# A Mamba block beside a mixture of experts: z projections between dt projections, and eight buffers for the products with C

## The chip, the cores and the metric

One core of one Trainium2 chip. The metric is the time in microseconds (us) of one execution on the device, the median of the runs. Engines by their names in the profile: PE (TensorE, matmuls), PEld (its weight loads), DVE (VectorE), ACT (ScalarE), POOL (GpSimd), SP (SyncE, which issues most of the transfers).

## What is computed

Input x is 2 x 512 tokens of 256 values. With xn the normalised x, the output is x + mamba(xn) + moe(xn), all in fp32.

```python
xz = xn @ in_proj_w.T                      # 1024 columns
x, z = split(xz)                           # 512 channels each
u = silu(conv4(x) + conv_b)
dt, Bm, Cm = split(u @ x_proj_w.T)         # 128, 16, 16 columns
dt = softplus(dt @ dt_proj_w.T + 2 * dt_proj_b)
h[l, n] = exp(dt[l] * A[n]) * h[l-1, n] + dt[l] * Bm[l, n] * u[l]    # 16 states n
y = (sum_n h[l, n] * Cm[l, n] + u * D) * z
mamba = y @ out_proj_w.T

p = softmax(xn @ gate_w.T)                 # 64 experts, the best 8 of each token
moe = sum over the 8 of p_e * (silu(xn @ w1_e.T) * (xn @ w3_e.T)) @ w2_e.T
```

## The kernel before

The 512 channels of the two sequences make 8 groups g of 128 channels by 512 steps (G = 8). Each group has 16 states, and a state is one scan over a 128x512 tile. Experts are worked in 128 tiles of 128 slots: tokens are scattered to their slots in slot_x, each tile is multiplied with its expert's weights, results go to slot_y and are gathered back. The order on each engine is written by hand, and engines wait for counters (semaphores) that other engines raise; `then_inc` raises one as an instruction ends, `wait_ge` waits. Some counters start C = 2 (or, cb_ok, K = 8) high.

**Head.** Norm, router, input projection, convolution, then u. GpSimd scatters 64 pieces of 128 rows from x_sb to slot_x by indirect transfers (L308). SP loads B and C rows into bc (L232) and then the first weight tiles (L242).

**dt and z.** TensorE computes eight dt projections (L850, banks 4 to 7, dt_ps counts them), two records of the trace each, then waits for the last of them to be used, then eight z projections (L858, also banks 4 to 7, four records each; z_ps counts each). ScalarE does for each group Abs (L667), Exp (L669) and a sum "+ 1" (L671), later Ln (L674), then it copies z to SBUF (L678), waiting for z_ps (L676) and for VectorE's softplus counter sp_v (L677), and after that begins the decays exp(dt A) of group 0 (`decay`, L687). VectorE does the maximum with zero (`over_zero`, L463), a rounding correction (`rounded`, L467) and three steps a group of `softplus` (L471, L473, L475).

**Group 0.** VectorE runs a scan (L501), forms the next state's input (`spread_u`, L494) and the product of the state with C (`times_c`, L508) for each state (`pair0`). TensorE adds the products into bank 0 with an identity matrix (`sum_states`, L872) and raises acc_ok by one for each. There are two product buffers, so L506 waits in each state for acc_ok of the state two before. After 14 sums and the last z copy TensorE goes on to the experts (`tile_slot`).

**Groups 1 to 5 beside the experts.** Expert tiles run through TensorE, ScalarE (tanh L710, copies L701, L704) and VectorE (`hidden`, L523 and L526), scans run between them, and GpSimd forms inputs (L316) and adds products in pairs (hp, L323). SP loads weights (`load_w`, L242) into the eight buffers w_buf and tokens (`load_x`, L245) into x_buf. The first x load waits until the whole scatter has landed (scat).

**Groups 6 and 7 (the tail).** VectorE goes back to `pair0` with two buffers. GpSimd gathers 64 pieces from slot_y (L349); from tile 4 on it waits for cb_ok. ScalarE builds eight diagonal matrices of weights a tile (L778, each behind cb_ok) and copies finished outputs (`output`, L766). TensorE sums states, combines the gathered rows with the diagonals (`combine`, L963, cb_ok counts each matmul) and does the output projection (L968). `finish_group` (L514, L516) waits for all 16 sums of a group. At the very end VectorE combines the last 128 tokens in eight steps (L629).

## Time and profile before

| | us |
|---|---|
| median of 3 runs | 599.52 |
| the three runs | 599.52, 605.4, 594.88 |
| span of the profiled execution | 596.5 |
| busy in that span: PE, DVE | 439.8, 452.3 |
| busy: POOL, ACT | 301.8, 271.5 |

The page gives the profiled execution's span, from the first to the last instruction, and no other time of its own; the median of the runs lies 3.0 us above the span. Times in the rows below count from the span's start. Busy time of POOL includes its indirect transfers' issue. "remote", "another core or an unknown queue" and "issue" stand where the profile can't name who ended a wait.

### The profile page before, as it was taken

How to read it: one execution, taken by the hardware profiler on the slowest of the kernel's cores; microseconds unless marked ns; L12 is line 12 of the kernel's file. 1: busy time of each engine (PE TensorE's matmuls, PEld its weight loads, DVE VectorE, ACT ScalarE, POOL GpSimd, SP SyncE). 2: the span in 40 equal slices, each digit the busy share in tenths (PEclk: the TensorE clock that was granted, in tenths of full speed). 3: DMA queues.
4: the chain of work that ended last, by engine and by line, in shares of the span. 5: the costliest groups of instructions: out<-in, count | busy, mean ns of one | idle time of the engine just before them, and what ended most of it. 6: DMA issues, size and time to landing. Idle time of an engine off the chain costs nothing.

```text
span 596.5 us, 10167 instructions
## 1 busy us (share of the span) xinstructions
PE 439.8 (74%) x2116; PEld 304.9 (51%) x2116; DVE 452.3 (76%) x870; ACT 271.5 (46%) x668; POOL 301.8 (51%) x260
## 2 busy tenths in 40 slices
PE   2987856200768888788889888899989958268888
PEld 2632222000115766667677776687777725135555
DVE  5476478001999999999989999788888889259786
ACT  1334690003223555555556666466555623134443
POOL 2003777771004555555554341667767667737750
PEclk9978967755677999999999999899999979768989
DMA  8995797423003899988989899699989443313331
GB/s 303 427 425 238 245 405 268 151 106 110 14 0 115 267 271 279 297 268 283 276 286 294 277 293 300 211 294 304 331 271 327 148 150 103 100 53 106 101 93 35
DMA packets 71642, 131.65 MB, mean 221 GB/s; under 512 B 7584, under 2 KB 44704, under 8 KB 69568
## 3 DMA queue, kind: packets, MB, share of 16 engines
q1 hardware_dynamic: 65472, 114.56, 57.7%
q0 software_dynamic: 6144, 16.79, 8.7%
q8 instruction: 11, 0.18, 0.1%
q14 instruction: 15, 0.12, 0.1%
HBM read 88.00 MB, written 43.32 MB: 220 GB/s over the span
## 4 chain that ended last, share of the span: by engine, by line
DVE 29%; PE 24%; issue 19%; another core or an unknown queue 9%; POOL 7%; ACT 7%; DVEq 2%; DMA 2%; POOLq 1%; SPq 0%; ACTq 0%
DVE bank L501 13%; POOL hp L323 5%; DVE hc L508 5%; PE bank L872 3%; PE bank L897 3%; PE bank L906 3%; DVE gt L523 3%; PE bank L808 2%; PE bank L914 2%; POOL dbu L316 2%; PE bank L968 2%; PE bank L963 2%; DVE wdt L526 2%; ACT dA L687 1%
## 5 line engine op out<-in xcount | busy, mean ns | idle before, releaser
L501 DVE TENSOR_TENSOR_SCAN bank<-dA,dbu 128x512 f32<-128x512 f32 x128 | 173.8, 1358 | 52.8 <-ACT dA L687 43.5
L316 POOL TENSOR_TENSOR dbu<-dtu,bc 128x512 f32 x80 | 102.0, 1276 | 173.4 <-DVE bank L501 162.0
L687 ACT ACTIVATE dA<-dt_sb,a_neg 128x512 f32 (+1 forms) x128 | 93.3, 729 | 92.9 <-DVE bank L501 62.7
L872 PE MATMUL bank<-hc,ident 128*128 128x512 f32 x92 | 64.8, 794 | 72.3 <-DVE hc L508 52.0
L508 DVE TENSOR_TENSOR hc<-bank,bc 128x512 f32<-128x512 f32 x128 | 87.6, 685 | 32.0 <-remote 20.6
L308 POOL DMA_INDIRECT slot_x<-x_sb,slot x64 | 64.0, 1000 | 68.8 <-DMA slot_x<-bc 49.6
L701 ACT COPY x_sb<-bank 128x256 f32<-128x256 f32 x128 | 47.7, 373 | 104.0 <-PE bank L906 87.7
L323 POOL TENSOR_TENSOR hp<-hc 128x512 f32<-128x512 f32 x41 | 67.3, 1642 | 3.9 <-DVE hc L508 3.8
L872 PEld LDWEIGHTS bank<-hc,ident 128*128 128x128 f32 x92 | 18.5, 232 | 99.3 <-DVE hc L508 73.7
L897 PE MATMUL bank<-x_sb,wring 128*128 128x128 f32 x512 | 68.1, 276 | 0.0
L897 PEld LDWEIGHTS bank<-x_sb,wring 128*128 128x128 f32 x512 | 62.7, 193 | 0.0
L906 PE MATMUL bank<-wring,wdt 128*128 128x256 f32 x128 | 40.6, 399 | 22.0 <-DVE wdt L526 21.3
L704 ACT COPY x_sb<-bank 128x256 f32<-128x256 f32 x128 | 48.4, 378 | 0.1
L526 DVE SCALAR_TENSOR_TENSOR wdt<-gt,bank 128x128 f32<-128x128 f32 x128 | 37.0, 289 | 13.5
L710 ACT ACTIVATE th<-bank 128x128 f32<-128x128 f32 x128 | 35.5, 278 | 20.1 <-PE bank L897 19.8
L914 PE MATMUL bank<-hp,ident 128*128 128x512 f32 x82 | 42.9, 606 | 1.1 <-POOL hp L323 1.1
L906 PEld LDWEIGHTS bank<-wring,wdt 128*128 128x128 f32 x128 | 21.7, 192 | 36.5 <-issue 33.1
L523 DVE SCALAR_TENSOR_TENSOR gt<-th,bank 128x128 f32<-128x128 f32 x128 | 35.2, 275 | 2.2 <-ACT th L710 2.0
L858 PE MATMUL bank<-xT,win 128*128 128x512 f32 x32 | 20.9, 817 | 18.8 <-issue 18.8
L897 PE MATMUL bank<-x_sb,win 128*128 128x128 f32 x256 | 34.7, 280 | 0.0
L897 PE MATMUL bank<-x_sb,xT 128*128 128x128 f32 x256 | 33.8, 275 | 0.0
L494 DVE TENSOR_TENSOR dbu<-dtu,bc 128x512 f32<-128x512 f32 x48 | 32.4, 675 | 0.5 <-DVE dtu L475 0.5
(137 smaller groups left out, 709.7 us busy)
## 6 DMA issues: line engine op xcount, KB each, us to landing
wring<-w_moe SPq DMA_DIRECT2D x64, 384.0 KB
slot_y<-x_sb SPq DMA_DIRECT2D x65, 256.0 KB, 4.8
slot_x<-bc SPq DMA_DIRECT2D x16, 1024.0 KB, 22.2
xT<-w_moe SPq DMA_DIRECT2D x32, 384.0 KB, 4.1
win<-w_moe SPq DMA_DIRECT2D x31, 384.0 KB, 4.6
bc<-bc_dram SPq DMA_DIRECT2D x8, 1024.0 KB
xg<-slot_x SPq DMA_DIRECT2D x32, 256.0 KB, 4.7
xT<-slot_x SPq DMA_DIRECT2D x16, 256.0 KB, 4.8
```

Of the source, the lines that this page charges most:

```text
L308: pool.indirect_dma_start(slot_x, bass.IndirectOffsetOnAxis(ap=slot[:, t * K + k:t * K + k + 1], axis=0), x_sb[:, t, :], None).then_inc(sc ...
L316: nc.gpsimd.tensor_tensor(dbu[:, j], at(dtu, g), bc[:, bass.ds(n, 1), 0].rearrange("p a l -> p (a l)"), ALU.mult).then_inc(dbu_ok, 1)
L323: nc.gpsimd.tensor_tensor(hp[:], hc[:, 0], hc[:, 1], ALU.add).then_inc(hp_ok, 1)
L501: nc.vector.tensor_tensor_scan(H[:], dA[:, j], dbu[:, j], 0.0, ALU.mult, ALU.add).then_inc(scan_ok, 1)
L508: nc.vector.tensor_tensor(hc[:, j], H[:], bc[:, bass.ds(n, 1), 1].rearrange("p a l -> p (a l)"), ALU.mult).then_inc(hc_ok, 1)
L523: nc.vector.scalar_tensor_tensor(gt[:], th[:, j], 1.0, GU[j][:, 0:INTER], ALU.add, ALU.mult).then_inc(gt_ok, 1)
L526: nc.vector.scalar_tensor_tensor(hh[:, w], gt[:], 0.5, GU[j][:, INTER:2 * INTER], ALU.mult, ALU.mult).then_inc(hh_ok, 1)
L687: nc.scalar.activation(dA[:, j], at(dt_sb, g), ACT.Exp, scale=a_neg[:, bass.ds(g, 1), bass.ds(n, 1)].rearrange("p a l -> p (a l)")).then_i ...
L872: nc.tensor.matmul(Y_ACC[:], ident[:], hc[:, j], start=first, stop=True, skip_group_check=True).then_inc(acc_ok, 1)
L897: mm = nc.tensor.matmul(GU[1 - j][:, half * P:(half + 1) * P], w_buf[w][:, k * 2 * P + half * P:k * 2 * P + (half + 1) * P], xTs[:, 1 - j, ...
L906: nc.tensor.matmul(YT[:, 0:DM], hh[:, w % 4], w_buf[w][:, WGU:], start=True, stop=True).then_inc(ye_ok, 1)
L914: nc.tensor.matmul(Y_ACC[:], ident[:], hp[:], start=(g is not None), stop=True, skip_group_check=True).then_inc(acc_ok, 2)
```

## The change

1. z projections are put between the dt projections: after dt 0 to 3, TensorE does z 0, dt 4, z 1, dt 5, z 2, dt 6, z 3, dt 7, then z 4 to 7. They go to banks 0, 1, 2, 3, 1, 2, 4, 5. z_ps is raised for z 0 to 3 one by one, and once, by four, after z 7.
2. ScalarE copies z 0 to 3 behind the Exp of groups 4 to 7, and z 4 to 7 behind the decays of states 2 to 5 of group 0. The "+ 1" sum goes from ScalarE to VectorE (`plus_one`). ScalarE starts group 0's decays after softplus of groups 0 and 1. The exponentials sp_e live in dA and in the weight ring, since z_sb keeps their old place.
3. Eight product buffers in groups 0, 6 and 7. In group 0 they are six parts of the weight ring and the two of hc; at the end hc, xg, prob, mask, key and a part of the ring. TensorE raises acc_ok by four after every fourth sum. VectorE waits for acc_ok once in four states (states 8 and 12 of groups 0 and 6, every fourth of group 7), for the sum four to eight states back. The loops over pairs in groups 6 and 7 are unrolled.
4. SP's first four weight loads wait for z_ps (their buffers are now the first ones of xT and win), and weight load 4 waits for the 14 sums of group 0.
5. The diagonals are doubled (two sets of eight), so ScalarE builds a tile's diagonals behind cb_ok of the tile two before. VectorE and ScalarE wait for the experts' last results before group 6 uses xg and the ring.

```diff
+        w_all = wring[:].rearrange("p a b -> p (a b)")
+        diag = w_all[:, 0:2 * K * P].rearrange("p (k q) -> p k q", k=2 * K)
+        whole = [w_all[:, i * L:(i + 1) * L] for i in range(6)]
+        sp_e = [dA[:, 0], dA[:, 1]] + whole
+        hc_first = whole + [hc[:, 0], hc[:, 1]]
...
-        w_buf = [wring[:, i] for i in range(4)] + [f[:, i * WCOL:(i + 1) * WCOL] for f in free for i in range(2)]
+        w_buf = [f[:, i * WCOL:(i + 1) * WCOL] for f in free for i in range(2)] + [wring[:, i] for i in range(4)]
...
+            sp.wait_ge(z_ps, G)
             for i in range(4):
                 load_w(i, i, False)
-            sp.wait_ge(z_ps, G)
+            sp.wait_ge(acc_ok, NS - 2 + C)
             load_w(4, 4, False)
...
+            def plus_one(g):
+                dve.wait_ge(sp_x, g + 1)
+                nc.vector.tensor_scalar(sp_l[:, g], sp_e[g], 1.0, None, ALU.add).then_inc(sp_s, 1)
...
-            def times_c(g, n, j, alone=True):
+            def times_c(g, n, j, ring=None):
                 s = g * NS + n
-                if alone:
-                    dve.wait_ge(acc_ok, s + C - 1)
                 dve.wait_ge(scan_ok, s + C + 1)
...
-            def pair0(g, q, count, after=None):
+            def pair0(g, q, count, ring, after=None):
                 for j in range(2):
                     n = 2 * q + j
+                    if n % PART == 0 and (n >= RING or g == G3):
+                        dve.wait_ge(acc_ok, g * NS + n - RING + PART + C)
...
+            dve.wait_ge(t_ok, TILES)
+            dve.wait_ge(ye_ok, TILES + 2 + C)
+            pair0(G2, 0, NS, hc_end)
...
-                act.wait_ge(sp_x, g + 1)
-                nc.scalar.activation(sp_l[:, g], sp_e[:, g], ACT.Copy, bias=1.0).then_inc(sp_s, 1)
+                if g >= 4:
+                    keep_z(g - 4)
...
-            act.wait_ge(sp_v, SP_STEPS * G)
+            act.wait_ge(sp_v, SP_STEPS * 2)
...
             for n in range(NS):
                 decay(0, n, n % 2)
+                if 2 <= n < 6:
+                    keep_z(n + 2)
...
+                        if t:
+                            act.wait_ge(cb_ok, (t - 1) * K + k + 1)
+                        nc.scalar.activation(diag[:, t % 2 * K + k], ident[:], ACT.Copy, scale=c8[:, t, k:k + 1]).then_inc(dg_ok, 1)
...
+            def project_z(g):
+                d, b = g % DT, g // DT
+                if g == 2:
+                    pe.wait_ge(bc_row, 1)
+                if g == 3:
+                    pe.wait_ge(split, 2)
+                if 4 <= g < 6:
+                    pe.wait_ge(z_ok, g - 2)
+                if g >= 6:
+                    pe.wait_ge(dt_max, g - 1)
...
+                if g < 4:
+                    mm.then_inc(z_ps, 1)
+                if g == G - 1:
+                    mm.then_inc(z_ps, 4)
+            for g in range(4):
+                project_dt(g)
+            for g in range(4):
+                project_z(g)
+                project_dt(4 + g)
+            for g in range(4, G):
+                project_z(g)
...
+                mm = nc.tensor.matmul(Y_ACC[:], ident[:], ring[n % RING], start=(n == 0), stop=True, skip_group_check=True)
+                if count:
+                    mm.then_inc(acc_ok, count)
             for n in range(NS - 2):
-                sum_states(0, n, n % 2, n == 0)
+                sum_states(0, n, hc_first, PART if n % PART == PART - 1 else 2 if n == NS - 3 else 0)
```

## Rows read from the trace of the kernel before

**Rows 1.** The chain that ended last, 82 to 150 us: start, length, what.

```profile
101.47 9.82 issue
...
111.31 11.14 another core or an unknown queue
...
141.40 2.08 another core or an unknown queue
```

**Rows 2.** The timeline: start us, length us, engine, line; in brackets idle time before, releaser.

```profile
82.41 13.39 PE L858 MATMUL bank<-xT,win 128*128 128x512 f32 x24 [6.41 <-issue]
...
100.08 0.59 ACT L678 COPY xpad<-bank 128x512 f32<-128x512 f32 x1 [9.92 <-remote]
...
111.93 3.71 PE L858 MATMUL bank<-xT,win 128*128 128x512 f32 x4 [7.43 <-issue]
```

**Rows 3.** The timeline of DVE from its first softplus step to its first scan.

```profile
84.93 0.69 DVE L471 TENSOR_TENSOR dtu<-dtu,xpad 128x512 f32<-128x512 f32 x1 [1.32 <-ACT dtu L674]
...
101.99 0.69 DVE L494 TENSOR_TENSOR dbu<-dtu,bc 128x512 f32<-128x512 f32 x1 [0.53 <-DVE dtu L475]
146.21 1.23 DVE L501 TENSOR_TENSOR_SCAN bank<-dA,dbu 128x512 f32<-128x512 f32 x1 [43.53 <-ACT dA L687]
```

**Rows 4.** Line 308, the scatter: shortest, median, longest ns; first and last start us.

```profile
L308 POOL DMA_INDIRECT slot_x<-x_sb,slot x64: 959/963/1630, 53.3 to 135.6; - x64
```

**Rows 5.** The timeline where the experts begin, 144 to 189 us.

```profile
144.21 0.34 SPq L242 DMA_DIRECT2D xT<-w_moe  x1
...
181.71 2.07 PE L872 MATMUL bank<-hc,ident 128*128 128x512 f32 x2 [0.47 <-DVE hc L508]
...
188.37 0.27 DVE L523 SCALAR_TENSOR_TENSOR gt<-th,bank 128x128 f32<-128x128 f32 x1
```

**Rows 6.** The timeline of the tail, 481 to 590 us.

```profile
481.03 1.23 DVE L501 TENSOR_TENSOR_SCAN bank<-dA,dbu 128x512 f32<-128x512 f32 x1 [1.15 <-POOL hp L323]
...
507.98 1.13 PE L872 MATMUL bank<-hc,ident 128*128 128x512 f32 x2 [0.42 <-issue]
...
519.86 0.69 DVE L508 TENSOR_TENSOR hc<-bank,bc 128x512 f32<-128x512 f32 x1 [10.09 <-remote]
...
588.73 4.12 DVE L629 SCALAR_TENSOR_TENSOR x_sb<-dtu,c,x_sb 128x256 f32<-128x256 f32 x8
```

**Rows 7.** DVE's waits, 481 to 588 us: us in total, times, longest us.

```profile
DVE hc L508 <- remote: 20.6, 3, 10.1
```

**Rows 8.** The timeline of the first dt projections.

```profile
65.11 4.53 PE L850 MATMUL bank<-hc,wdt 128*128 128x512 f32 x10
```

**Rows 9.** Groups of lines, 66 to 102.5 us: count, busy us, mean ns, idle before.

```profile
L463 DVE TENSOR_SCALAR dt_sb<-bank,dtb 128x512 f32<-128x512 f32 x8 | 6.0, 750 | 6.3 <-issue 6.3
...
L467 DVE SCALAR_TENSOR_TENSOR xpad<-dtu,xpad 128x512 f32<-128x512 f32 x8 | 5.4, 682 | 0.0
...
L671 ACT ACTIVATE dtu<-xpad 128x512 f32<-128x512 f32 x8 | 5.0, 630 | 0.3
```

**Rows 10.** DMA issues: KB each, median us from issue to landing.

```profile
xg<-slot_x SPq DMA_DIRECT2D x32, 256.0 KB, 4.7
```

**Rows 11.** The timeline of GpSimd's scatter.

```profile
86.02 1.17 POOL L308 DMA_INDIRECT slot_x<-x_sb,slot  x1 [0.30 <-issue]
...
102.59 0.96 POOL L308 DMA_INDIRECT slot_x<-x_sb,slot  x1 [0.30 <-issue]
...
126.67 0.96 POOL L308 DMA_INDIRECT slot_x<-x_sb,slot  x1 [0.30 <-issue]
```

**Rows 12.** GpSimd's gathers in 482 to 581 us, two of four rows.

```profile
L349 POOL DMA_INDIRECT xT<-slot_y,slot_r x16 | 18.1, 1131 | 14.8 <-PE bank L963 8.7 <-issue 4.3 <-DVE dbu L494 1.8
...
L349 POOL DMA_INDIRECT dt_sb<-slot_y,slot_r x16 | 15.7, 981 | 4.9 <-issue 4.9
```

**Rows 13.** The timeline of GpSimd's gathers, ten of them.

```profile
497.43 0.95 POOL L349 DMA_INDIRECT win<-slot_y,slot_r  x1 [0.30 <-issue]
...
508.70 1.24 POOL L349 DMA_INDIRECT dt_sb<-slot_y,slot_r  x1 [0.30 <-issue]
```

83 lines of the change are left out of this document (40 added, 43 removed).

## The prediction

> **What bounds the kernel now.** I read the chain of waits first, then the timeline of single engines where the chain names no releaser, then grouped rows for prices. The span is 596.5 us, and the median of three runs is 599.5 us; I work on the span and add the 3.0 us between the two at the end.
>
> The chain has a hole at the front. From 101.47 to 143.5 us it is made of five waits ahead of ScalarE's z copies (L678), four of them put down to an unknown queue [rows 1]. The timeline shows what is waited for. TensorE had six of the eight z projections done by 82.41 + 13.39 = 95.8 us, the last at 111.93 + 3.71 = 115.6 us; the copies after the second start at 100.08, 111.29, 122.48, 132.28, 141.37 and 143.50 us, nine to eleven us apart until the last one (three of the five pieces of the chain stand in rows 1) [rows 1, 2]. ScalarE waits at L676 for z_ps, which TensorE counts up, and L677's counter, VectorE's, stood complete at 101.5 us. So a count that TensorE owed at 92 to 96 us is seen 19 to 36 us late. VectorE had all its softplus work done at 101.5 and its first dbu ready at 102.7, and then stood 43.5 us until the first decay (L687), which ScalarE issues behind the copies [rows 3]. What works in those 43.5 us is GpSimd's scatter, whose 64 transfers run from 53.3 to 136.6 us [rows 4]. SP too sat on z_ps, for weight load 4, until 144.21 [rows 5].
>
> The same thing comes back in the tail. Groups 6 and 7 run from 481.03 us at one state per 2.54 us, while GpSimd gathers. VectorE's product (L508) waits three times, 20.6 us in all, the longest 10.09 us with TensorE's matmul (507.98 + 1.13 us) long over [rows 6, 7]. L506 waits there for acc_ok, again a count of TensorE's. Between the two, from 188 to 481 us, the change touches nothing.
>
> **The change part by part.** I take as the mechanism that, once GpSimd's indirect transfers have run for 26 (tail) to 39 us (front), counts that TensorE sends are seen about 10 us late, one after the other. Counts of the first 30 us of the scatter (the dt projections from 65.11 us on) were prompt [rows 8].
>
> Step 1, z between dt. A dt projection is two records at 0.45 us each (ten records in 4.53 us) at a granted clock near full; a z projection is four, so 1.8 us, or 3.7 us at half clock [rows 2, 8]. Four z's between the eight dt's end dt 7 at about 65.1 + 8 x 0.9 + 4 x 1.8 = 79.5 us, where its Abs is due at about 80, so it costs 0. At half clock it is 65.1 + 8 x 1.8 + 4 x 3.7 = 94, some 11 us later than the softplus can bear; I take full clock, since TensorE would have no gap to lose it in, and keep 11 us as bound. All eight z's then end at 87 to 90 us, inside the time in which counts were prompt. ScalarE loses eight sums of 0.63 us and gains four copies of 0.59; VectorE gains the eight sums, at most 0.68 us each like its other pass [rows 2, 9]. VectorE then has 8 x (0.75 + 0.68 + 0.68) = 16.9 us of work from 67.0 us, with a start-up gap of 1.3, thus 85 us; its first softplus step began at 84.93 before [rows 3]. Zero.
>
> Step 2, group 0 moves forward. The decays wait for two softplus groups only, and four z copies are laid behind decays 2 to 5, where ScalarE is idle for over a microsecond in each state. The first scan then starts at 102.7 instead of 146.21 us. State 13's sum started 181.71 - 146.21 = 35.5 us after the first scan [rows 3, 5]; so now at 138.2, done at 140.3.
>
> Step 3, late counts in group 0. Eight buffers and one count in four states: state 8 needs the count of state 3. That matmul ends at about 114; with the 10.6 us of the z copies it is seen at 124.8 against a need at 102.7 + 8 x 2.54 = 123.0. States 12 and 7 meet likewise. I charge 3 us in all (bounds 0, and 2 x 11 us if the counts queue behind others). State 13 is summed by 143.3.
>
> Step 4, the start of the experts. They need the scatter complete, state 13's count on SP (new), then weight load 4 and x loads: 0.4 + 0.5 us of issue and 4.7 us to land [rows 5, 10]. The scatter runs at 1.267 us a transfer with VectorE idle (102.59 to 126.67, 19 steps) and at 1.381 beside the softplus (86.02 to 102.59, 12 steps) [rows 11]. 26 transfers beside the scans cost 26 x 0.114 = 3.0 us: the last lands at about 141. After it the counts are prompt within 2 us, as for the last z copy [rows 2], so SP goes on at 145 and x is there at 150.5. The first gate product (L523) follows the transposes by 1.8 us: 152.3. It started at 188.37 before, held then by VectorE's own group 0 [rows 5]. Gain 36 us. Bounds: 40 if no count is late (148.2), 27 if state 13's count takes a full 11.2 us. SP's four first weight loads move behind z_ps; they were 8.4 us apart before and are needed at 150, so 34 us from 90 fit.
>
> Beside the scatter's pace the Trainium skill, SBUF — State Buffer, section "SBUF: two separate sides", has a rule against this change: while VectorE runs a two-port mode, GpSimd can't write the descriptors of its transfers. The moved sum (tensor_scalar, fp32, SBUF to SBUF) may be of that kind. By the rule eight such instructions hold up the scatter by their own length, 8 x 0.68 = 5 us; by the pace of rows 11 it is 8 x 0.114 = 0.9 us, and the sum holds neither.
>
> Step 5, the tail. Without the 20.6 us of waits on acc_ok and some 1 us of small ones the last eight-step sum (L629) could start at 588.73 - 21.6 = 567.1 [rows 6]. GpSimd then becomes the limit: 64 gathers, in four rows of 16, are 18.1 + 17.3 + 16.4 + 15.7 = 67.5 us of work and 4.3 + 4.9 + 4.6 + 4.9 = 18.7 us of issue [rows 12], so 482.84 + 86.2 = 569.0, and 1.4 us to land as the scatter's last: 570.4. At its fast pace, 1.25 us (497.43 to 508.70, nine steps) [rows 13], it would be 564. I take 570.4: gain 18.3. What stays late: ScalarE still waits four times for cb_ok ahead of output copies (L774) and VectorE for acc_ok in finish_group, each with only two states, 5 us, of slack against a count that can be 10 us late; five spots, late at the rate of three in 32 states, 5 us each, make 2.3; I charge 3. Gain 15 (bounds: 5 if most of the 20.6 us only moves to those spots, 21 if nothing is late and the gathers keep their fast pace). The unrolled loops and the doubled diag cost nothing: group 0 was unrolled before and keeps 35.5 / 14 = 2.54 us a state, as the loops do; diag gains four states of slack. The waits for ye_ok and t_ok ahead of group 6 are met at 480.0, before GpSimd's hp sum, which held the scan until 481.03 [rows 6].
>
> Sum: 36 + 15 = 51; 596.5 - 51 = 545.5 of span, 548.5 us. What measurement of this kernel tells from no change is about 2%, 12 us.
>
> **The rivals.**
> (a) The counts queue. If TensorE's counts pass one in 10 us while GpSimd's transfers run, eight combine counts and one acc count per four states pile up in the tail, and group 0 waits at 8 and at 12. For it: the even distance of the z copies [rows 1]. Against it: only three late counts were waited for in 100 us of tail, which has over 90 of them [rows 7]. Front gain 27, tail 8: 564.5 us.
> (b) It is not TensorE's count that is late but ScalarE and VectorE that are held by the scatter. Then group 0 can't run beside it, the front gains nothing, the tail stays or gains its 18: 581 to 599 us. Against it: VectorE worked through its softplus to 101.5 us at full pace beside the scatter, and copies were late when z_ps was their only open wait. In a sentence apart: the Trainium skill, TensorE: Matmul & The Clock Gate, section "The cost: per-tile semaphore tail", puts counts that queue up at 26 ns each; by that figure fewer counts save 2 us here at most and (b) is what is left, yet the trace shows 9 to 11 us each.
> (c) It ends slower: GpSimd's issue is thinned out by a VectorE that never pauses, to one transfer per state, 2.54 us. The scatter's last 26 transfers then take 26 x (2.54 - 1.38) = 30 us more, and 64 gathers take 163 us instead of 86, 77 more: 548.5 + 30 + 77 = 655.5 us. It decides from a pace of about 1.95 us (at p us a transfer the gains are 176 - 90 p). Against it: the nine steps at 1.25 us stood beside scans at full cadence [rows 13].
> (d) Half clock in step 1: softplus 11 us later, first scan at 113.6, state 13 summed at 151 and promptly counted, x at 157. Gain 30: 554.5, inside the forecast's own range.
>
> **How the numbers follow.** Forecast 548.5 us, own range 540 to 560, chance 0.62, (d) included. (a) 0.20, to 568. (b) 0.07. (c) 0.03. Left over 0.08, mostly below 540. The range 538 to 568 takes the bounds 40 + 21 = 61 us and 27 + 5 = 32 us of gain and leaves out (b), (c) and a little. Faster by over 2%: 0.94; within: 0.03; slower: 0.03.
>
> **What would show it.** Right: first scan at about 103 us; the four late z copies at single spots of group 0; scatter over by about 140; first gate product at 150 to 155; from there to the first scan of group 6 the same 292.7 us; no wait over 3 us at the products; last gather at about 569, L629 close behind. Step 3 is wrong if state 8 or 12 waits for over 5 us; step 4 if x is there well before or after 150; step 5 if output copies or combine hold ScalarE, or GpSimd's gaps grow. The whole is wrong if the first scan still waits for the scatter's end.

## The result, and the profile after

| | kernel before | changed kernel |
|---|---|---|
| median | 598.36 us (4 executions, 594.88 to 605.40) | 572.75 us (4 executions, 567.82 to 586.70) |
| profiled execution | span 596.5 | 567.82, span 565.9 |
| first scan of group 0 | 146.21 | 104.03 |
| first gate product | 188.37 | 163.62 |
| first scan of group 6 | 481.03 | 458.00 |
| last eight-step sum of rows (L629, now L648) | 588.73 | 558.17 |

The ratio is 0.9531, 95% interval [0.9447, 0.9615]: 4.7% faster, where 8.5% was forecast (548.5 us), and the median lies above the range of 538 to 568. Ratios leave out executions more than 1.5% above the fastest one of the same kernel; since such executions turn out to be part of the story, the range of all of them stands beside each median.

The profiled execution is the fastest of the four; no profile shows where the others lost the 3 to 19 us more. Of the 51 us forecast it has 30.6 (596.5 - 565.9): 24.8 at the front (188.37 - 163.62) instead of 36, 7.5 in the tail (107.7 - 100.2) instead of 15, and 1.7 lost in the middle (292.7 and 294.4 us). So the missing 20 us are 11.3 at the front, 7.5 in the tail and 1.7 between.

The front of the changed kernel, timeline (start, length, engine, line; in brackets the idle time before and its releaser):

```profile
73.98 1.02 PE L875 MATMUL bank<-hc,wdt 128*128 128x512 f32 x2
74.84 7.03 PE L890 MATMUL bank<-xT,win 128*128 128x512 f32 x16
...
120.24 2.04 PE L916 MATMUL bank<-wring,ident 128*128 128x512 f32 x2 [5.26 <-DVE wring L523]
```

```profile
81.37 0.69 ACT L691 ACTIVATE wring<-bank,dtb 128x512 f32<-128x512 f32 x1 [5.93 <-issue]
...
101.93 1.28 ACT L707 ACT_TABLE_LOAD   x1 [13.15 <-DVE dtu L487]
...
116.39 0.58 ACT L686 COPY xpad<-bank 128x512 f32<-128x512 f32 x1 [10.29 <-remote]
```

```profile
104.03 1.23 DVE L517 TENSOR_TENSOR_SCAN bank<-dA,dbu 128x512 f32<-128x512 f32 x1 [1.05 <-issue]
...
117.69 1.23 DVE L517 TENSOR_TENSOR_SCAN bank<-dA,dbu 128x512 f32<-128x512 f32 x1 [6.17 <-issue]
...
138.80 1.23 DVE L517 TENSOR_TENSOR_SCAN bank<-dA,dbu 128x512 f32<-128x512 f32 x1 [7.30 <-issue]
...
163.62 0.29 DVE L538 SCALAR_TENSOR_TENSOR gt<-th,bank 128x128 f32<-128x128 f32 x1 [2.93 <-ACT th L732]
```

Read them by pairs. The last dt projection ended at 75.0, and ScalarE's Abs of it started at 81.37, 5.93 us after ScalarE had come to it: 6.4 us behind its sum. The last z ended at 81.87 (74.84 + 7.03) and its copy started at 116.39: 34.5 us behind. ScalarE's copy holds the decay behind it, so the fourth scan stands 6.17 us. State 3's sum ended at 122.28 and state 8's scan, which waits for its count, started at 138.80: 16.5 us behind. The z copies that held the kernel before for 43.5 us [rows 1 to 3] are gone, but late counts now stop the front at three places. It isn't the waiting engine that is slow. SP waits for the same count of z 7, and its first instruction behind that wait, the value load of L246, starts at the same instant as ScalarE's copy (the view of line 246: shortest, median and longest ns; first and last start):

```profile
L246 SPq TENSOR_LOAD <-tile_e x127: 263/272/960, 116.4 to 439.1; - x127
```

SP's queue in the timeline:

```profile
121.25 8.42 SPq L249 DMA_DIRECT2D xT<-w_moe  x2
136.66 7.72 SPq L249 DMA_DIRECT2D win<-w_moe  x2
156.85 0.34 SPq L249 DMA_DIRECT2D wring<-w_moe  x1
157.25 0.93 SPq L252 DMA_DIRECT2D xg<-slot_x  x2
```

Weight load 4 waits for state 13's count and the x load (L252) is issued behind it, at 157.25, though the scatter had been over since 140.8 (its last transfer, 139.00 + 1.79). SP's queue is the chain by which 14.8 us of stopped scans become a late expert.

The tail, waits from 458 us on (total, times, longest), and the timeline where they stand:

```profile
ACT x_sb L789 <- remote: 18.2, 2, 11.6
...
DVE bank L517 <- ACT dA L707: 10.9, 2, 8.0
...
DVE u L529 <- PE bank L916: 5.1, 1, 5.1
```

```profile
505.88 0.37 ACT L789 COPY x_sb<-bank 128x256 f32<-128x256 f32 x1 [11.60 <-remote]
...
540.35 0.37 ACT L789 COPY x_sb<-bank 128x256 f32<-128x256 f32 x1 [6.59 <-remote]
```

The first line reads: ScalarE stood 18.2 us in all ahead of L789, in two waits, the longest 11.6 us. VectorE's 20.6 us at the products [rows 7] are gone. What is late next are two output copies, 18.2 us of ScalarE, of which 10.9 reach the scans, and the last sum's count, 5.1.

### The profile page after: what moved, and what is told of

Its sections match the earlier page's. It is cut to its first block, busy times and chain, and to the rows that moved or that the text cites. A ratio compares the mean times of both kernels' runs of the same rounds, so it can differ in the third digit from the quotient of the medians.

```text
span 565.9 us, 10023 instructions
## 1 busy us (share of the span) xinstructions
PE 429.2 (76%) x2116; PEld 300.2 (53%) x2116; DVE 453.1 (80%) x878; ACT 264.8 (47%) x660; POOL 302.8 (54%) x260
## 4 chain that ended last, share of the span: by engine, by line
DVE 32%; PE 24%; issue 17%; ACT 9%; DMA 4%; another core or an unknown queue 3%; POOL 3%; SPq 3%; DVEq 2%; ACTq 0%; POOLq 0%
DVE bank L517 12%; PE bank L943 5%; PE bank L952 5%; DMA slot_y<-x_sb 3%; ACT dA L707 3%; DVE gt L538 3%; POOL hp L331 3%; PE bank L960 3%; DVE dbu L510 2%; PE bank L1009 2%; DVE hc L523 2%; PE bank L832 2%; DVE wdt L541 2%; DVE wring L523 2%
## 5 line engine op out<-in xcount | busy, mean ns | idle before, releaser
L324 POOL TENSOR_TENSOR dbu<-dtu,bc 128x512 f32 x80 | 101.8, 1274 | 143.4 <-DVE bank L517 132.0
L316 POOL DMA_INDIRECT slot_x<-x_sb,slot x64 | 67.0, 1047 | 70.1 <-DMA slot_x<-bc 50.8
L723 ACT COPY x_sb<-bank 128x256 f32<-128x256 f32 x128 | 47.6, 372 | 102.5 <-PE bank L952 86.1
L523 DVE TENSOR_TENSOR hc<-bank,bc 128x512 f32<-128x512 f32 x92 | 63.1, 686 | 9.0 <-POOL hp L331 8.8
L943 PE MATMUL bank<-x_sb,wring 128*128 128x128 f32 x512 | 69.8, 281 | 0.0
L943 PEld LDWEIGHTS bank<-x_sb,wring 128*128 128x128 f32 x512 | 64.5, 198 | 0.0
L916 PE MATMUL bank<-wring,ident 128*128 128x512 f32 x32 | 27.7, 963 | 44.6 <-issue 33.9
L952 PE MATMUL bank<-wring,wdt 128*128 128x256 f32 x132 | 42.7, 406 | 15.8 <-DVE wdt L541 14.8
L916 PEld LDWEIGHTS bank<-wring,ident 128*128 128x128 f32 x32 | 7.2, 274 | 62.4 <-issue 52.7
L952 PEld LDWEIGHTS bank<-wring,wdt 128*128 128x128 f32 x132 | 22.7, 196 | 30.6 <-issue 25.4
L952 PE MATMUL bank<-win,wdt 128*128 128x256 f32 x64 | 20.7, 405 | 15.7 <-DVE wdt L541 15.4
```

Source lines behind the costliest of these rows:

```text
L316: pool.indirect_dma_start(slot_x, bass.IndirectOffsetOnAxis(ap=slot[:, t * K + k:t * K + k + 1], axis=0), x_sb[:, t, :], None).then_inc(sc ...
L324: nc.gpsimd.tensor_tensor(dbu[:, j], at(dtu, g), bc[:, bass.ds(n, 1), 0].rearrange("p a l -> p (a l)"), ALU.mult).then_inc(dbu_ok, 1)
L523: nc.vector.tensor_tensor(ring[n % RING] if ring else hc[:, j], H[:], bc[:, bass.ds(n, 1), 1].rearrange("p a l -> p (a l)"), ALU.mult).the ...
L943: mm = nc.tensor.matmul(GU[1 - j][:, half * P:(half + 1) * P], w_buf[w][:, k * 2 * P + half * P:k * 2 * P + (half + 1) * P], xTs[:, 1 - j, ...
L952: nc.tensor.matmul(YT[:, 0:DM], hh[:, w % 4], w_buf[w][:, WGU:], start=True, stop=True).then_inc(ye_ok, 1)
```

## The experiments

Each kernel ran beside the kernel before, on the same chip. Where texts of the first batch number their theories, 1 is that TensorE's counts are held while GpSimd's indirect transfers run (later, in its strict form with one count leaving after the other, Q), and 3 that a TensorE that idles sends its counts late. This table of the profiled executions carries most of what follows. "Middle" is from the gate product to group 6, "tail" from there to the last sum of rows (us).

| kernel | first scan | gate product | middle | tail |
|---|---|---|---|---|
| before | 146.2 | 188.4 | 292.7 | 107.7 |
| changed | 104.0 | 163.6 | 294.4 | 100.2 |
| e1_z_one | 113.6 | 168.5 | 294.1 | 100.3 |
| e2_hold_scatter | 98.2 | 226.5 | 293.7 | 98.8 |
| e3_front_alone | 99.9 | 151.4 | 296.1 | 105.2 |
| e4_tail_alone | 144.3 | 186.4 | 295.9 | 99.0 |
| e5_acc_each (no late count) | 99.8 | 146.3 | 295.1 | 87.5 |
| e6_z_late (no late count) | 100.8 | 146.4 | 296.1 | 87.5 |
| e7_scatter_pause (no late count) | 99.7 | 153.3 | 294.2 | 87.5 |
| e8_out_late (no late count) | 101.1 | 148.2 | 294.7 | 87.5 |
| f1_after_again (the changed kernel) | 140.3 | 184.6 | 293.6 | 100.2 |
| f2_combined | 101.9 | 152.1 | 297.3 | 96.1 |
| g1_dt_first | 107.3 | 182.0 | 297.1 | 99.3 |
| g2_dt_combined | 97.4 | 151.9 | 295.1 | 100.7 |
| g3_many_counts | 97.2 | 154.6 | 296.0 | 102.3 |
| g4_dt_pause | 100.0 | 155.0 | 296.7 | 99.3 |
| h1_before_pause | 101.8 | 154.3 | 296.0 | 112.0 |
| h2_pauses_combined | 99.8 | 149.2 | 296.8 | 99.1 |
| i1_more_stops | 100.4 | 152.8 | 296.5 | 99.4 |
| i2_after_stops (the kernel of e7) | 100.8 | 153.1 | 294.9 | 99.9 |

The middle is within 5 us everywhere; all is decided in front and tail.

**e1_z_one.** Is it the size of the raise (four at once behind z 7)?

```
-                if g == G - 1:
-                    mm.then_inc(z_ps, 4)
+                if g == G - 1:
+                    mm.then_inc(z_ps, 1)
```
(with waits for 5 instead of 8.)

> The changed kernel, but the count after z 7 is one instead of four (ScalarE, SP and GpSimd wait for 5). In the changed kernel the last z matmul ended at 81.9 us and the count was seen at 116.3 us, 34.4 us late; a raise by four may be worked off as four raises of 8.6 us. Theory 1 (TensorE's raises pass one at a time, 8 to 11 us each, while GpSimd's indirect transfers run, and a raise by four is four of them): the copy of z 4 starts by about 92 to 106 us, right behind its decay, the 6.2 us gap of VectorE ahead of state 3 goes, and the time falls by 4 to 8 us against the changed kernel. Theory 2 (a raise is late by itself, whatever its size): the copy still starts at about 116 us, time as the changed kernel within 2 us.

573.58 us (569.35 to 585.83), ratio 0.9546 [0.9499, 0.9593]: as the changed kernel. z 4's copy still waited 12.51 us, to 128.91. The size of a raise is not the cause.

**e2_hold_scatter.** The scatter waits until group 0 has been summed.

```
             pool.wait_ge(rt, RT_SLOT)
+            pool.wait_ge(acc_ok, NS - 2 + C)
```

> The changed kernel, but GpSimd begins its scatter only when the 14 sums of group 0 are counted. Theory 1 (counts are late because of GpSimd's indirect transfers): z 4's copy starts right behind decay 2, all 16 states of group 0 follow each other at 2.54 us with no gap over 0.5 us, state 8 waits for nothing. The scatter then runs from about 140 to 222 us, so the whole takes 60 to 70 us longer than the changed kernel, about 635 us. Theory 3 (a count of TensorE's is late because TensorE stands idle behind it): the copy of z 4 is again some 30 us behind the last z matmul and state 8 waits again, with no transfer of GpSimd's in flight.

628.75 us, since the experts start 38 us later than before. But in front nothing is late: the dt copies wait 0.5 and 0.8 us, the scans start at 98.17 and run through, although TensorE idles as before. So an idle TensorE is not enough for a late count, and with GpSimd's transfers gone the late counts went too. It is one execution; h1 below rests on four. Nor is it the load of the DMA engines as such: in e2 they were busy throughout from 70 to 80 us (387 GB/s), beside dt counts in time, and in the changed kernel z 7's count stayed out from 90 to 110 us while they were busy for 26 to 36%.

**e3_front_alone and e4_tail_alone.** The change cut in two: e3 keeps the tail of before (two buffers, a count for each sum, one set of diagonal matrices), e4 is the kernel before with the tail's three edits.

```
e3 +        hc_end = 4 * [hc[:, 0], hc[:, 1]]
e3 +                if ring is hc_end:
e3 +                    dve.wait_ge(acc_ok, s + C - 1)
...
e4 +                mm = nc.tensor.matmul(Y_ACC[:], ident[:], ring[n % RING], start=(n == 0), stop=True, skip_group_check=True)
e4 +                if count:
e4 +                    mm.then_inc(acc_ok, count)
```

> The changed kernel with the tail as before: two product buffers and a count per state in groups 6 and 7, one set of diagonals. The profiles of before and after put 24.8 us of the gain in front of the first gate product and 7.5 us behind the first scan of group 6. If the parts add up: about 24 us under the kernel before, 7 us over the changed kernel, with late waits of 15 to 22 us at the products of the tail. If the front's gain is given back later: within 10 us of the kernel before.

> The kernel before with only the tail of the change: eight product buffers, a count in four states and doubled diagonals in groups 6 and 7. If the parts add up: 7 to 8 us under the kernel before; the products wait for nothing, and the late counts show at the output copies of ScalarE instead (two waits, 18 us in the changed kernel) and at the decays. If the ring alone did what was forecast: 15 us or more under.

e4 took 591.93 us (589.55 to 594.67), 0.9877 [0.9837, 0.9918]: the tail is worth some 8 us, with the same two output copies in the way (18.2 us, the longest 11.6). Its front is that of before, and so are its z copies, timelines of TensorE and ScalarE:

```profile
81.72 15.19 PE L870 MATMUL bank<-xT,win 128*128 128x512 f32 x28 [6.41 <-issue]
```

```profile
102.36 0.59 ACT L688 COPY xpad<-bank 128x512 f32<-128x512 f32 x1 [10.62 <-issue]
...
133.86 0.59 ACT L688 COPY xpad<-bank 128x512 f32<-128x512 f32 x1 [9.92 <-remote]
```

Seven z projections (28 records) were over at 96.9 us. The copies of z 3 to z 6 started at 102.36, 112.86, 123.36 and 133.86: four counts that TensorE owed by 96.9 were seen one at a time, 10.5 us apart. e3 took 579.97, but from 562.30 to 601.17, and in its profiled execution (562.30) the front had almost no late count at all: gate product at 151.4, as forecast for the whole change (152.3). The executions of this one kernel lie up to 39 us apart; what was late in the slower ones no profile shows.

**e5_acc_each, e6_z_late, e7_scatter_pause, e8_out_late.** One edit each on the changed kernel: a count per state in group 0 with a wait for state n - 8 alone; z 4 to 7 copied behind decays 10 to 13; three stops in the scatter; output copies a tile later.

```
e5 -                sum_states(0, n, hc_first, PART if n % PART == PART - 1 else 2 if n == NS - 3 else 0)
e5 +                sum_states(0, n, hc_first, 1)
e6 -                if 2 <= n < 6:
e6 -                    keep_z(n + 2)
e6 +                if 10 <= n < 14:
e6 +                    keep_z(n - 6)
e7 +                if t in (2, 4, 6):
e7 +                    pool.wait_ge(scat, 16 * t * K)
e8 -                    if i == 1 and 1 <= t <= 4:
e8 -                        act.wait_ge(cb_ok, t * K + K)
e8 -                        output(t - 1)
e8 +                    if i == 0 and 2 <= t <= 5:
e8 +                        act.wait_ge(cb_ok, t * K)
e8 +                        output(t - 2)
```

> Group 0 of the changed kernel with TensorE's count raised once per state again (16 counts instead of four); state n from 8 on waits for the sum of state n - 8 alone, not for a group of four. Theory Q (counts of TensorE leave one at a time, about one per 10 us, while GpSimd's indirect transfers run, so each further count makes the later ones later): after z 7's count at about 116 the counts of states 0, 1, 2 come at about 126, 136, 140 to 143, so VectorE stops at states 9 to 11 for 10 us or more in all, and the first gate product comes no earlier than 163. Theory L (a count is late by some time, up to 16 us here, however many there are): the sum of state n - 8 has then 20 us of slack in place of 12.7, VectorE's 7.3 us wait ahead of state 8 goes, ScalarE's wait for z 7 stays, and the first gate product comes at 156 to 158; time 564 to 569 us.

> The changed kernel with ScalarE's four copies of z 4 to 7 behind the decays of states 10 to 13 instead of 2 to 5: nothing of the scans stands behind z 7's count before 130 us. If the late z count cost what the trace shows (6.2 us of scans), VectorE runs on until state 8; there it waits for the count of state 3's sum. If that count comes by its own time (theory L, some 16 us behind its sum, which now ends at about 114), at 130: state 8's scan would stand at about 124.5, so 5 us of waiting and a first gate product at 155 to 157. If it comes when GpSimd's transfers end (139, theory E), state 8 waits 14 us and the gate product stays at 162 to 164: no gain. SP's weight loads behind z 7's count stay late in both. Time 564 to 568 by L, 572 by E.

> The changed kernel with GpSimd waiting, ahead of its 17th, 33rd and 49th indirect transfer, until all earlier ones have landed: three stops of some 2 to 3 us, the scatter's end at 146 to 149 instead of 141. If counts of TensorE pass when GpSimd stops (as they do in the tail, where eight of them land within 0.4 us, 3 us behind GpSimd's stop), z 7's count comes at about 100 and the sum of state 3's is at hand for state 8: ScalarE's 10.3 us and VectorE's 7.3 us waits shrink to under 2 us each, the scans end at about 146, and the scatter's end sets x: first gate product at 155 to 158, time 564 to 569 us. If they don't pass in so short a stop, both waits stay and the end of the scatter adds to them: gate product at 164 or later.

> The changed kernel with ScalarE's output copies of tiles 0 to 3 one tile of states later in the tail (behind the decay of state 4t + 10 in place of 4t + 7 or so: slack of seven states in place of four, 7.6 us more; the two projections that need the bank follow two states later). If the copy's wait for late counts is what holds the scans in the tail (VectorE's 8.0 and 2.9 us), it shrinks to 0 to 4 us in all and the tail from the first transfer of the gather to the last multiply by z is 7 to 11 us shorter: time 562 to 566 us. If another wait takes its place at once (the diagonal matrices' own for the counts, with one state less of slack, or GpSimd's for free rows), it moves under 3 us: 570 to 573 us.

None of these expectations came true, for a reason that none had: in the four profiles of this batch no count was late, and the kernel before took 536.57 us (24 executions, 534.15 to 539.39) instead of 599. The changed kernel itself was not in this batch, but three kernels one edit away from it: e5, e6 and e8 took 538.52, 538.24 and 538.94, ratios 1.0028, 1.0030 and 1.0029 (each interval within 1.000 to 1.006). The scans of e5_acc_each, timeline of VectorE:

```profile
99.79 1.23 DVE L517 TENSOR_TENSOR_SCAN bank<-dA,dbu 128x512 f32<-128x512 f32 x1 [1.05 <-ACT dA L710]
...
137.92 1.23 DVE L517 TENSOR_TENSOR_SCAN bank<-dA,dbu 128x512 f32<-128x512 f32 x1
141.72 2.02 DVE L517 TENSOR_TENSOR_SCAN bank<-dA,dbu 128x512 f32<-128x512 f32 x1 [1.84 <-ACT dA L710]
146.32 0.29 DVE L538 SCALAR_TENSOR_TENSOR gt<-th,bank 128x128 f32<-128x128 f32 x1 [2.58 <-ACT th L735]
```

Sixteen scans at 2.54 us with no gap, then the scatter's end. So all that can be measured of the change's gain, it gains on late counts; where there are none, these three are 0.3% behind the kernel before. The batch ran on a chip on which a later batch (i1, i2) had the kernel before at 606 us: the lateness is a property neither of a chip nor of the program alone. What switches it on I can't say. e7's stops were 5.0, 1.7 and 1.7 us, and it took 543.21 us, 4.7 more than e5.

**f1_after_again and f2_combined.** The changed kernel once more, and the edits of e5, e6 and e8 together.

> The changed kernel, nothing edited, once more beside the kernel before. The last four kernels ran with the kernel before at 536.6 us, 62 us under the time it had in the first two batches, and no count of TensorE was late in any of their profiles; the lateness belongs to something outside the program. If this batch's chip has late counts (kernel before near 598), the changed kernel takes 568 to 576. If it has none (kernel before near 537), VectorE runs without a stop from the first scan to the last in both kernels, the change takes nothing off its path and the two are within 0.5%: 535 to 540.

> The edits of three kernels together, on the changed kernel: one count per state in group 0 with the wait for state n - 8 alone, ScalarE's copies of z 4 to 7 behind the decays of states 10 to 13, output copies one tile later in the tail. Where counts are late: by theory L (a count is late by a time of its own) the front loses 6 and 7 us of waits and the tail 7 to 11, 550 to 557 us against 568 to 576 of the changed kernel. By theory Q (counts leave one by one, 10 us apart, while GpSimd's transfers run) the sixteen counts of group 0 stop VectorE at states 9 to 11 and the front gains nothing: 562 to 568. Where no count is late: 535 to 540, as without the edits.

f1 took 588.12, 586.92, 586.10 and 556.60 us: the same kernel is 11 to 13, or 43, us faster than before (599.45). f2: 554.08, then 572.68, 574.09 and 585.14. The profiled execution of f1 is the slowest (588.12); timeline of ScalarE:

```profile
83.62 0.69 ACT L691 ACTIVATE wring<-bank,dtb 128x512 f32<-128x512 f32 x1 [10.13 <-remote]
97.62 0.69 ACT L691 ACTIVATE wring<-bank,dtb 128x512 f32<-128x512 f32 x1 [12.18 <-remote]
114.43 0.69 ACT L691 ACTIVATE wring<-bank,dtb 128x512 f32<-128x512 f32 x1 [14.98 <-remote]
137.66 1.28 ACT L707 ACT_TABLE_LOAD   x1 [15.84 <-DVE dtu L487]
```

These are the Abs of dt 5, 6 and 7, whose sums ended at 71.5, 74.1 and 76.7 us: counts 12, 24 and 38 us late, seen one at a time, 14 and 17 us apart, with the first scan at 140.32. The softplus of all groups stands behind them, and the decays behind that. The kernel before had no such wait in its profile: its dt counts were all raised ahead of any z. In f2's profiled execution they were on time (one of 3.2 us), and no scan of states 1 to 15 waited over 1.2 us.

**g1_dt_first to g4_dt_pause.** g1 undoes the interleaving, with what hangs on it: z 3 raises z_ps by four, and ScalarE copies z 0 to 3 ahead of the decays. g3 adds seven counts to it, on a counter that nobody waits for; g4 adds stops; g2 adds f2's edits. The cut shows the order on TensorE and the line of g3.

```
g1 -        Z_BANK = [PS[i] for i in (0, 1, 2, 3, 1, 2, 4, 5)]
g1 +        Z_BANK = PS[0:G]
...
g1 -            for g in range(4):
g1 -                project_dt(g)
g1 -            for g in range(4):
g1 -                project_z(g)
g1 -                project_dt(4 + g)
g1 -            for g in range(4, G):
g1 -                project_z(g)
g1 +            for g in range(G):
g1 +                project_dt(g)
g1 +            for g in range(G):
g1 +                project_z(g)
g3 +                    if g > 3 and k < KD - 1:
g3 +                        mm.then_inc(spare, 1)
```

> The changed kernel with one part undone: the eight dt projections first, the eight z behind them (each z with a bank of its own, one count of four behind z 3 and one behind z 7; ScalarE copies z 0 to 3 ahead of the decays and z 4 to 7 behind decays 2 to 5 as in the change). Theory Q (late counts leave in order, one every 5 to 15 us, from some point between 68 and 80 us on): with only the dt counts ahead, dt 7's is at hand by 73, no copy of a dt projection waits, the scans start at about 100 in every run, and the spread of the changed kernel (556 to 588) goes: all runs at 555 to 572. Theory S (the spread comes from somewhere else, interleaving z has no part in it): times of 556 to 588 again, and Abs waits of 6 to 15 us in some profiles. Where no count is late: 536 to 541.

> dt first as in g1_dt_first, with the three edits of f2_combined (a count per state in group 0, z 4 to 7 copied behind decays 10 to 13, output copies one tile later). f2_combined had 554.1 in the execution whose dt counts were in time and 573 to 585 in the others. Theory Q: here all are of the first sort, 548 to 556. Theory S: 554 to 585 again.

> g1_dt_first with seven more counts: each of the eight matmuls of z 4 to 7 but the last also raises a semaphore that nobody waits for. Theory Q: the seven stand ahead of z 7's count in the queue, which then comes when the scatter ends (141 or later) instead of between 90 and 120; ScalarE's copy of z 4 waits to then, VectorE stops after state 3, and the first gate product is 20 us or more later than in g1_dt_first: 580 to 600 us. Theory L (a count is late by a time of its own, whatever number is raised): no difference from g1_dt_first. Where no count is late: 536 to 541.

> g1_dt_first with GpSimd waiting ahead of its 17th, 33rd and 49th scatter transfer until all earlier ones have landed. On a chip without late counts the same stops were 5.0, 1.7 and 1.7 us and cost 5 to 7 us. If held counts pass in such a stop, ScalarE's wait for z 7 and VectorE's ahead of state 8 are under 3 us each, and the end of the scatter (147 to 149) sets x: first gate product at 155 to 158. If they don't pass, both waits stay as in g1_dt_first, and it is slower than that by 3 to 8 us.

g1: 562.58 us, but 556.41, 558.21 and 562.58 beside 587.76 and 588.11, so the spread stayed, against theory Q as I had put it. No Abs of a dt projection waited over 1.1 us in its profile; there (588.11) z's two counts took over, timelines of TensorE and ScalarE:

```profile
73.76 13.90 PE L888 MATMUL bank<-xT,win 128*128 128x512 f32 x32
```

```profile
103.09 2.05 ACT L686 COPY xpad<-bank 128x512 f32<-128x512 f32 x4 [19.16 <-remote]
143.01 0.59 ACT L686 COPY xpad<-bank 128x512 f32<-128x512 f32 x1 [33.68 <-remote]
```

z 7 had ended at 87.7 and its count came at 143.0, behind the scatter's last transfer, 55 us late, though only two counts were raised for all eight z. g3, with seven more raised ahead of z 7's, should have been worse. It took 562.00 (558.80 to 562.93), and the copy of z 4 stood 1.1 us:

```profile
100.40 0.58 ACT L686 COPY xpad<-bank 128x512 f32<-128x512 f32 x1 [1.11 <-remote]
```

The count had come 16 us late (z 7 ended at 84.4). It came 16.4 us behind z 3's (the copies behind that started at 84.03), with the seven in between. So counts do not pass at a fixed 10 us each, and theory Q falls as I had put it. What stays open is whether a counter with nobody waiting counts in full here. VectorE also stood 10.97 us in this profile, at 139.76, for a sum's count. g4, with stops: 560.55, all four within 560.20 to 563.49, and no late count in front; its gate product (155.0) waits for the scatter's end. g2: 557.06 (554.53 to 560.15), 0.9285 [0.9205, 0.9364], with more slack in place of stops, and none of its executions is among the late ones either.

**h1_before_pause.** The kernel before, and only GpSimd's three stops:

```
             for t in range(NT):
+                if t in (2, 4, 6):
+                    pool.wait_ge(scat, 16 * t * K)
                 for k in range(K):
```

> The kernel before with one edit: GpSimd waits ahead of its 17th, 33rd and 49th scatter transfer until all earlier ones have landed. g4_dt_pause had no late count in the front at all with these stops. If held counts pass in each stop, and none is held for some 15 us behind one, the five copies of z that each waited about 10 us [the stretch from 88 to 144 us of the kernel before] come within 25 us: first scan at 112 to 125 instead of 146, first gate product at 155 to 168 instead of 188, time 567 to 580 us: with two lines of the kernel changed, most of what the whole change brought. If stops help only where few counts are in use (the kernel before has 8 of z and 16 of group 0, each waited for at once), 590 to 600. On a chip without late counts: 537 to 543.

572.50 us (571.11 to 573.98), 0.9511 [0.9446, 0.9577]: with two lines, what the whole change brought (0.9531), and steadier (four executions within 2.9 us, where the changed kernel's lay 19 us apart). GpSimd's stops, and the places where the kernel before had stood 43.5 us, timeline:

```profile
81.13 1.32 POOL L310 DMA_INDIRECT slot_x<-x_sb,slot  x1 [5.04 <-DMA slot_x<-x_sb,slot]
...
104.52 1.90 POOL L310 DMA_INDIRECT slot_x<-x_sb,slot  x1 [1.71 <-DMA slot_x<-x_sb,slot]
```

```profile
90.52 0.58 ACT L680 COPY xpad<-bank 128x512 f32<-128x512 f32 x1 [1.13 <-DVE dt_sb L475]
92.24 0.58 ACT L680 COPY xpad<-bank 128x512 f32<-128x512 f32 x1 [1.13 <-PE bank L860]
```

```profile
149.54 2.39 DVE L503 TENSOR_TENSOR_SCAN bank<-dA,dbu 128x512 f32<-128x512 f32 x1 [7.46 <-issue]
154.34 0.29 DVE L525 SCALAR_TENSOR_TENSOR gt<-th,bank 128x128 f32<-128x128 f32 x1 [2.40 <-ACT th L712]
```

The z copies are 1.7 to 2.1 us apart, the pace of TensorE's projections and VectorE's softplus, where they were 10 [rows 1]. The first scan is at 101.82, two us ahead of the changed kernel's, and the gate product at 154.34, nine ahead. This is the cleanest proof that the unbroken run of transfers is the cause. Whether a stop helps because GpSimd pauses or because no transfer of its is then on the way, no run separates. One stop at 76 to 81 us is enough for all z counts to 98 us to be prompt. Its tail, which has no stop, is as before or worse (112.0), with one product waiting 15.56 us.

**h2_pauses_combined, i1_more_stops, i2_after_stops.** h2 is g2 with one stop in the scatter and two in the gather; i1 is g2 with two and five; i2 is the changed kernel with the scatter's three, the same kernel as e7_scatter_pause. The cut shows the stops in the gather.

```
h2 +                if t in (2, 6):
h2 +                    pool.wait_ge(g_ld[1], (t // 4 + 1) * 16 * K)
i1 +                if t in (2, 3, 5, 6, 7):
i1 +                    pool.wait_ge(g_ld[(t - 1) % 4], ((t - 1) // 4 + 1) * 16 * K)
```

> g2_dt_combined with three stops of GpSimd: one in the scatter (ahead of its 33rd transfer) and two in the gather of the tail (ahead of the 17th and the 49th), each until the earlier transfers have landed. g2_dt_combined's tail from the first transfer of the gather to the last sum of rows was 98.9 us, 85.7 on a chip without late counts. If stops of 2 to 5 us release the counts held in the tail, VectorE's 6.5, 1.7 and 6.4 us waits there go and the tail is 89 to 94 us; the stop in the scatter costs its 2 to 3 us at the front: 549 to 554 us. If the end of the gather sets the tail, its stops add to it: 558 to 563.

> g2_dt_combined with stops of GpSimd ahead of the 17th and 33rd transfer of the scatter and ahead of each tile of the gather from the third on. In h2_pauses_combined a count raised at 488.9 passed at 506.0, with GpSimd's next stop: here a stop comes every 10 to 12 us of the gather, so no wait on a late count is over 10 us and the 13.3 us one goes; five stops of 2 us put the gather's end at 90 to 94 us behind its start. Tail from its first transfer to the sums of rows 90 to 95 us (h2_pauses_combined: 97.3), time 546 to 552 us. If the counts don't come out in each stop, 553 to 558.

> The changed kernel, its dt and z projections interleaved as they are, with the scatter's three stops alone. h1_before_pause (the kernel before with the same stops) had its first gate product at 154.3 and took 572.5. If the front's loss was late counts alone, dt counts included, the gate product stands at 153 to 157 here too, whatever the order of the projections, all runs lie within 6 us of each other and take 558 to 565 us: what the change is worth once the counts are on time is its tail alone, 8 to 12 us. If interleaving costs by itself, 568 or more, or a spread over 15 us.

h2: 553.76 us (551.91 to 557.07), 0.9199 [0.9127, 0.9272], the fastest median where counts are late. Its time lies in the expected 549 to 554, but not for the reason given: the tail hardly shortened (99.1 for g2's 100.7), the front did (149.2 for 151.9). In its tail one count shows how a release looks, timelines of TensorE, GpSimd and VectorE:

```profile
487.77 1.10 PE L916 MATMUL bank<-wring,ident 128*128 128x512 f32 x2 [0.65 <-issue]
```

```profile
506.32 0.95 POOL L361 DMA_INDIRECT win<-slot_y,slot_r  x1 [4.07 <-remote]
```

```profile
506.00 0.75 DVE L533 SCALAR_TENSOR_TENSOR u<-u,d_col,bank 128x512 f32<-128x512 f32 x1 [13.29 <-remote]
```

Group 6's last sum ended at 488.87. GpSimd stopped at 502.25, itself waiting for late combine counts, and at 506.0 VectorE and GpSimd both went on. i1 put a stop about every 12 us into the gather, and the late counts were gone from VectorE's path: no wait for a count there is over 1.3 us. The time was 555.88 (552.72 to 559.26), 0.9160 [0.9095, 0.9226], by its ratio no different from h2. It lies where the expectation had it if counts did not come out in the stops; they did, but the gather now ends last:

```profile
533.63 0.75 DVE L533 SCALAR_TENSOR_TENSOR u<-u,d_col,bank 128x512 f32<-128x512 f32 x1 [1.28 <-PE bank L916]
548.64 4.13 DVE L655 SCALAR_TENSOR_TENSOR x_sb<-dtu,c,x_sb 128x256 f32<-128x256 f32 x8 [13.54 <-DMA dtu<-slot_y,slot_r]
```

i2: 559.20 us (553.42 to 562.13), 0.9187 [0.9099, 0.9276]; with three stops alone the changed kernel can't be told from h2 and i1. Its profile catches a late count at a stop, timelines of ScalarE and GpSimd:

```profile
76.41 0.69 ACT L693 ACTIVATE wring<-bank,dtb 128x512 f32<-128x512 f32 x1 [4.02 <-PE bank L877]
```

```profile
79.33 0.95 POOL L318 DMA_INDIRECT slot_x<-x_sb,slot  x1 [4.76 <-DMA slot_x<-x_sb,slot]
```

dt 6's sum had ended at 72.8; GpSimd stopped from 74.57 to 79.33, and the Abs went on at 76.41, 1.8 us into the stop. The same kernel without late counts (e7) had its gate product at 153.3: three stops take away all that late counts cost in the front, at the price of the stops themselves (146.3 in e5, which has none), and what late counts still cost in the tail is 12.4 us (99.9 and 87.5). The time and the gate product are as expected, the spread is wider (8.7 us for 6). Its gate product, 153.1, is h1's within 1.2 us. So with prompt counts the front of the change brings nothing, and its tail 12.1 us (112.0 and 99.9); by the ratios to the kernel before, i2 is 3.2 points below h1. By their ratios i2, i1, h2, g4 and g3, and g2, are all better than the changed kernel (0.916 to 0.936 against 0.953).

## Why the prediction was wrong

**The bottleneck** was read rightly: counts of TensorE that come late while GpSimd scatters and gathers held the kernel before. h1 and e2 show it, and the batch without late counts shows the size: the kernel before took 536.57 us there, 62 less and lower than the 548.5 forecast for the change. Rival (b), ScalarE and VectorE held by the scatter, is refuted by h1, where both work beside it.

**The mechanism** ("once GpSimd's indirect transfers have run for 26 (tail) to 39 us (front), counts that TensorE sends are seen about 10 us late, one after the other") was wrong in its onset and its price. dt 5's sum ended 19 us into the scatter in f1, and its count was already 12 us late. In single executions z 7's was 16, 34.5 and 55 us late (g3, changed kernel, g1), and the same kernel took 556.6 and 588.1 us. Nor has each count a price of its own: seven more left z 7's 16 us late (g3), and one raise instead of four changed nothing (e1). What every late profile has is an uninterrupted run of GpSimd's indirect transfers. In the profiles read here, a late count was seen at the latest 2 to 7 us after GpSimd stopped (1.8 us in i2, 3.7 in h2's tail, 4.6 in g1 at 143.0 for an end at 137.46 + 0.96, 7.0 for z 7's of the kernel before at 143.50 for 135.55 + 0.96), but often in the middle of the run: z 7's of the changed kernel at 116.39, state 3's at 138.80.

"One after the other" is not refuted. In e4 four counts owed by 96.9 us passed 10.5 us apart, and in the kernel before z 3 to z 5, all summed by 95.8, were seen at 111.29, 122.48 and 132.28 [rows 1, 2]; no projection had to come in between. So the even spacing was real, twice. What sets it, 10 us there, 14 and 17 in f1, 16 for eight counts in g3, stays open. The error was to take the rate and the prompt first 39 us of one profile over to another order of work. ScalarE's own counts were prompt all the while: TensorE, waiting for the copy of z 2, which ended at 100.67, began z 6 at 100.72.

**Step 1** (z between dt, "Zero") failed, by its sentence "All eight z's then end at 87 to 90 us, inside the time in which counts were prompt". The arithmetic of the projections was good: they ran at full clock and ended even at 81.9. But the late counts began within them, 20 us into the scatter. dt 7's count was 6.4 us late in the profile after, and dt 5 to 7's were up to 38 us late in f1. In the former it ate what the shortened softplus had saved (g2 and g3, with dt first, scanned from 97.4 and 97.2 us), in the latter it moved the first scan to 140. With dt first no Abs waited over 1.1 us, in g1 neither. Putting dt first didn't by itself narrow the spread: in g1 the z counts took the same room. So whether this step gains or loses differs from execution to execution.

**Step 2** held: scan at 104.03, one state per 2.54 us between stops. It had overlooked that the decays wait for all the softplus, through VectorE's own start of the scan counter (the table load at 101.93, 13.15 us of waiting), worth 1.3 us at most.

**Step 3** (3 us, bounds 0 and 22) was mis-sized: the scans stood 6.17 + 1.36 + 7.30 = 14.8 us. It priced state 8's count at 1.8 and state 12's likewise; state 8 stood 7.30 and state 12 nothing. The 6.17 us of z 7's count ahead of decay 3 had no term, because step 1 had it prompt. The 1.36 us stand behind VectorE's own product, and no run shows why. (By the step's own rows state 3's matmul ends at 114.9, not 114.)

**Step 4** had the scatter's end right (140.8 for 141) and the x load wrong (157.25 for 145): not through the scatter, but because "state 13's count on SP (new)" made SP wait for scans which step 3 had at 143. The gate product followed at 163.62 instead of 152.3. An x load ahead of weight load 4 was not tried. The scatter took 84.5 us from first to last start, 82.3 before [rows 4]: 2.2 us more, where the sum had 0.9 and 3.0. The eight moved sums took 0.41 to 0.57 us each, 3.5 in all, where 0.68 each was priced, and GpSimd's 14 transfers beside them (66.16 to 84.92 us) took 1.0 us more than at 1.267 each. By the rule of the Trainium skill, SBUF — State Buffer, section "SBUF: two separate sides", such sums hold up GpSimd's transfers by their own length if they run in a two-port mode, an estimated 3.5 us. The trace, with 1.0, doesn't bear it out; whether they run in that mode it doesn't say.

**Step 5** (15 us, bounds 5 and 21) came out at 7.5 and named the spots itself: output copies and finish_group. It priced them at 5 us a spot times the old rate; two copies cost 10.9 and the last count 5.1. Moving the copies a tile later (f2, g2) took these waits away, but the tail was 96.1 and 100.7 us (100.2 without), the time going to the next count in line. Nor is GpSimd the limit that the step took, at 570.4: the gather took 89.7 us with its two waits for late counts; it sets the end only in i1. Without late counts the tail is 87.5.

**The rivals.** (a), at 564.5, came nearest in time and in its two terms (front 27, tail 8; measured 24.8 and 7.5), though counts did not pass at 10 us each. It should have had more than 0.20: its weight was set by "only three late counts were waited for in 100 us of tail", which counts waits, not late counts. (c), a thinned-out issue, didn't occur: 64 transfers at 1.27 us beside scans. (d), half clock, neither: the granted clock from 61 to 82 us was 1.00 of full speed, the level of 2.4 GHz. Its sum for (c) has a slip, 176 - 90 p for 173 - 90 p, on which nothing rests. And the 3.0 us added to the span are too many: in each run of the record the execution's time lies 1.8 to 2.1 us above its span (567.82 and 565.9 here). The other rule of the Trainium skill, TensorE: Matmul & The Clock Gate, section "The cost: per-tile semaphore tail", puts a count that queues at 26 ns. The batch without late counts doesn't contradict it: e5, with a count for each state of group 0, took 538.52 us and e6, with one in four, 538.24. The late counts are hundreds of times that.

## What to carry to other kernels

Waits of ScalarE, VectorE and SP that end together, with the TensorE work long over, while GpSimd issues indirect transfers without a break, point to late counts: try a stop of GpSimd (wait for its own transfers every 16) before any reordering; here two lines were worth 5%. Give each such count more slack than one observed lateness (they ranged from 6 to 55 us here), and keep SP's urgent loads from standing behind a weight load that waits for one. And when a gain rests on a disturbance that a single profile shows, take profiles of several executions: here it came and went between batches and between executions of one kernel.

## What the runs showed of the hardware that was not expected

- TensorE's semaphore counts came up to 55 us late during GpSimd's indirect transfers (g1), and were prompt in the front with no transfers (e2) and with a stop each 16 transfers (h1, g4, and i2 but for dt 6's, 3.6 us late and let go within a stop). In the kernel before and in e4 they came one at a time, some 10 us apart. The stops cost 1.7 us each once the first (5.0) was over.
- ScalarE's counts to TensorE were prompt in the same time (0.05 us, kernel before at 100.7).
- All of it was absent in one batch (kernel before 536.57 us) and present on the same chip later (605.98 us), 69 us apart.
- SP's weight loads beside the scatter were some 8 us apart (two issues in 8.42 and in 7.72 us), and 0.4 us behind its end. Whether from the same cause wasn't tried.
